# Moving four small loads to another engine's queue and reordering the first expert's loads in a LoRA mixture-of-experts kernel

## The chip, the cores and the metric

The kernel runs on one core of one Trainium2 chip. A core has TensorE (PE, with its weight loads as PEld), VectorE (DVE), ScalarE (ACT), GpSimd (POOL) and SyncE (SP); loads and stores are issued on the queues of SP, ACT and POOL and carried out by 16 DMA engines. The metric is the device time of one execution in microseconds (us); lower is better.

## The reference

The input is eight sequences of 256 rows of 256 numbers. Each goes through a gated retention layer against a context, and then through a mixture of eight experts, of which each row takes two:

```python
x = x + tanh(g_xattn) * xattn(layernorm(x), ctx, ctx, Wq, Wk, Wv)   # q, k rotated; (q k^T * decay) v
xf = layernorm(x)
gates = top2_normalised(softmax(xf @ Wg.T))                          # 8 experts, 2 per row
h1 = xf W1 + (xf A1) B1 + b1                                         # per expert, LoRA rank 16
h3 = xf W3 + (xf A3) B3 + b3
y_e = g W2 + (g A2) B2 + b2,   g = silu(h1) * h3
x = x + tanh(g_ffn) * sum_e gates_e * y_e
```

W1 and W3 are 512 x 256 per expert, W2 is 256 x 512, and the biases are drawn at random, so they count.

## The kernel before, in words

The kernel has two phases. In the **batch phase**, eight batch steps (`step(s, ...)` on each engine) compute the retention layer, one sequence per step. Beside it each step prepares the weights of one expert: the product of the LoRA factors is folded into the expert's weights. In the **tile phase**, 39 tiles of 128 gathered rows go through the experts (L617 to L644 on TensorE).

A step on TensorE (L519 to L571) has this order: keys of sequence s from its context `cx` (L529); from step 1 on the scores of s-1 (L493) and the first pair of fold products `units(0, 1)` (L471); the attention product (L514 to L516), which needs the masked scores `ret` that VectorE makes (L1213, L1214); transposes of the normalised rows `xn` (L482); fold products `units(2, 3)`; queries (L557); values (L566); fold products `units(4, 5)` (L475). Every engine runs its instructions in the order written, and so do the queues.

*The fold.* Each expert's weights come in six units of 128 x 512 (256 KB each), two per kind; the kinds 0, 1 and 2 are W1, W3 and W2. A unit lands in a `stage` buffer (L395), TensorE multiplies the LoRA rows `LS` (L471 or L475), VectorE adds the product to the stage (L1121), ScalarE rounds the sum into `WH` (L739), and GpSimd writes the rest into `WL` (L980). `LS[kind]` holds 48 LoRA rows (L387: 144 KB out of `WH`, where the split factors lie early on) and, for kinds 0 and 1, four rows that stand for the last weight row and the bias (L379) and, once, two unit rows (L372). A normalised row sums to zero, so the last weight row can be taken off all others, and a 1 in the last place carries the bias.

*The factors.* `lraw` is loaded kind by kind (`load_raw`, L413). VectorE subtracts the last column (L1169), ScalarE rounds into three parts (`round_factors`, L733 and L735), and rests are formed on VectorE (L1184, L1188) and GpSimd (L1006).

*The rows of last weights and biases.* Four loads of 16 KB (L420, L421: eight rows of 2 KB each) bring them into `last_raw`, 32 rows of 512. VectorE splits them into a rounded part and a rest, `last_rows` (`rows_of_last`, L1173 to L1178), at the end of its part of step 0.

*SyncE's queue* (L403 to L445) issues in this order: x and context of sequence 0, the projections and tables, `load_raw(0)`, a table, `load_raw(1)`, the four loads of last rows and biases, `load_raw(2)`, the mask, the gate weights, x and context of sequence 1, constants; then all six weight units of expert 0 (L429, L430); then, for each expert and kind, `load_factors` and (from expert 1 on) `load_weights`. `load_factors` makes the queue wait: for expert 0 on `s_last_rows` (L370), the unit rows, and the rounding and rests of this kind (L384 to L386); for later experts until TensorE is through with the LS buffer (L363). `load_weights` waits until GpSimd has freed the stage (L393).

*ScalarE* begins with the load of the two gate inputs (L709) and their tanh (L711), then the deviation of sequence 0 (L794, a square root), the normalised rows (L744), their transposes (L803). [...] It also loads x and context from sequence 2 on (L762, L763).

*GpSimd* clears the LS buffers and makes the unit rows (L990 to L1000), then takes its first step: key rotation (L985, L986), a factor rest, query rotation, another factor rest.

Of the kernel before, what the change touches and what calls it, by code (L numbers as in the profile page):

```python
# [25 lines left out]
F32 = mybir.dt.float32  # L26
# [52 lines left out]
def flamingo(nc, x, ctxT, wqkv, tables, mask, gates_in, w_all, lora, biases, wgT, ident_in, consts, out):  # L79
# [10 lines left out]
    with whole:  # L90
# [262 lines left out]
        def _(sp):  # L353
# [35 lines left out]
            def load_weights(s, u, kind):  # L389

                for m in (2 * kind, 2 * kind + 1):
                    n = s * UNITS + m
                    pos_wait(sp, s_wl, stage_last(n) + 1)  # L393
                    b = stage_of(n)
                    sp.dma_start(stage[b][:, :], w_all[s, m]).then_inc(s_stage[b], 16)  # L395

            def load_units(s, u, kind):

                load_factors(s, u, kind)
                if s > 0:  # L400
                    load_weights(s, u, kind)

            load_x(0)  # L403
            sp.dma_start(cx[0][:], ctxT[0]).then_inc(s_ctx[0], 16)
# [10 lines left out]
            load_raw(0)  # L415
            sp.dma_start(tab_q[:], tables[:, 0:2]).then_inc(s_qtab, 16)
            load_raw(1)
            for kind in range(2):
                rows = slice(2 * kind * E, 2 * (kind + 1) * E)
                sp.dma_start(last_raw[rows][0::2], w_all[:, 2 * kind + 1, P - 1, :]).then_inc(s_last_in, 16)  # L420
                sp.dma_start(last_raw[rows][1::2], biases[:, kind * HID:(kind + 1) * HID]).then_inc(s_last_in, 16)  # L421
            load_raw(2)
            sp.dma_start(msk, mask).then_inc(s_msk, 16)
            sp.dma_start(wg[:], wgT).then_inc(s_msk, 16)
# [3 lines left out]
            sp.dma_start(cst[:], consts).then_inc(s_cst, 16)  # L428
            for kind in range(KINDS):  # L429
                load_weights(0, 0, kind)  # L430
            for s in range(E - 1):
                for kind in range(KINDS):
                    load_units(s, s % 2, kind)

# [272 lines left out]
        @block.scalar  # L707
        def _(act):
            act.dma_start(gin[:], gates_in).then_inc(s_gin, 16)  # L709
            act.wait_ge(s_gin, 16)  # L710
            nc.scalar.activation(tg[:], gin[:], ACT.Tanh).then_inc(s_tg, 1)  # L711
            act.wait_ge(s_eps, 1)
# [264 lines left out]
        def _(pool):  # L977
# [20 lines left out]
            pool.wait_ge(s_unit_row, 2)  # L998
            nc.gpsimd.tensor_copy(unit_rows, unit_raw).then_inc(s_unit_row, 1)
            pool.wait_ge(s_unit_row, 3)  # L1000

            def factor_rest(kind):

# [111 lines left out]
        def _(dve):  # L1115
# [54 lines left out]
                dve.wait_ge(s_lsub, kind + 1)  # L1170
                nc.vector.memset(lraw[:, b - 1:b], 0.0).then_inc(s_ldiff, 1)

            def rows_of_last():  # L1173

                dve.wait_ge(s_last_in, 4 * 16)
                nc.vector.tensor_copy(last_rows[:, 0], last_raw).then_inc(s_last_hi, 1)
                dve.wait_ge(s_last_hi, 1)
                nc.vector.tensor_tensor(last_rows[:, 1], last_raw, last_rows[:, 0].bitcast(F32), ALU.subtract).then_inc(s_last_rows, 1)  # L1178

            def factor_rests(kind):  # L1180

                dve.wait_ge(s_lhi, kind + 1)
# [53 lines left out]
            def step(s, u, two, three):  # L1236
                b = s - 2
                weight = lambda m: add(s - 1, 1 - u, m)

                dve.wait_ge(s_kproj, s + 1)  # L1240
                pos_wait(dve, s_qT, 2 * s)
                rotate(pK, 2, 0)
                if s > 0:
                    variance(st1, mv1, s_mv1, early_sums[0])
                rotate(pK, 2, 1, s_krot)
                if s == 0:
                    lifted_factors(0)
                    lifted_factors(1)
                    factor_rests(0)
                else:  # L1250
                    dve.wait_ge(s_sd1, s + 1)
                    dve.wait_ge(s_xn, s)
                    shift(mv1, rs1, nm1, s_nm1, scale(sd1, rs1))
                if s == 1:
                    factor_rests(2)
                    dve.wait_ge(s_msk, 2 * 16)
                if two:
                    masked(s)
                    weight(0)
                    weight(1)  # L1260
                if three:
                    row_maxima(b, pL)
                    sorted_eight(b)
                    indices(b)
                if two:
                    if s == 1:
                        dve.wait_ge(s_tg, 1)
                    residual(s, xs[(s - 1) % XRING])
                    dve.wait_ge(s_x2, s)
                    n = sums(x2, st2)  # L1270
                    weight(2)
                    variance(st2, mv2, s_mv2, n)
                    weight(3)
                    if s == B - 1:
                        early_counts()
                    dve.wait_ge(s_sd2, s)
                    pos_wait(dve, s_xn2, s - 1)
                    shift(mv2, rs2, nm2, s_nm2, scale(sd2, rs2))
                if s == 0:
                    dve.wait_ge(s_qtab, 16)  # L1280
                dve.wait_ge(s_qproj, s + 1)
                dve.wait_ge(s_kT, 2 * (s + 1))
                rotate(pQ, 0, 0)
                rotate(pQ, 0, 1, s_qrot)
                if s == 0:
                    factor_rests(1)
                    rows_of_last()
                if s + 1 < B:
                    r = (s + 1) % XRING
                    dve.wait_ge(s_xload[r], 16 * ((s + 1) // XRING + 1))  # L1290
                    early_sums[0] = sums(xs[r], st1)
                    if two:
                        weight(4)
                        weight(5)
# [340 lines left out]
```

## Time and profile before

| | us |
|---|---|
| median of 3 runs | 327.74 (327.45 to 331.18) |
| the profiled execution | 328.52 |
| its span, first to last instruction | 326.7 |
| around the span | 1.8 |
| TensorE busy in the span | 297.4 (91%) |
| VectorE, ScalarE, GpSimd busy | 198.9, 203.5, 207.5 |
| mean granted TensorE clock | 0.968 of full |

Times in the rows are us from the start of the span. A busy TensorE is not TensorE at its peak, since matmuls are pipelined. The granted clock is 1.00 at 2.4 GHz and 0.50 at 1.2 GHz. "Idle before" is an engine's idle time ahead of an instruction, with what ended it; a q behind an engine's name (SPq, ACTq) means its sequencer, which issues loads.

### The profile page before, as it was taken

Reading aid. Unit: us, or ns where it says so; the run is one execution under the profiler, and the core shown is the slowest. Engines: PE = TensorE matmul, PEld = TensorE weight load, DVE = VectorE, ACT = ScalarE, POOL = GpSimd, SP = SyncE. Lnnn points to the kernel's source line nnn. Section 1 sums busy time; section 2 is a strip of 40 time slices with the busy share of each in tenths; the row PEclk is TensorE's granted clock in tenths of the full one; section 3 lists DMA queues with packets and bytes.
Section 4 is the critical chain, followed back from the end, with each engine's and each line's share of the span. In section 5 each row is a group of like instructions: output and inputs, shape, how many; then the busy total and the mean of one; then the engine's idle time right before and its main releaser. Section 6 shows DMA issues by size and latency. Waiting matters only on the chain.

```text
span 326.7 us, 7141 instructions
## 1 busy us (share of the span) xinstructions
PE 297.4 (91%) x1735; PEld 231.2 (71%) x1755; DVE 198.9 (61%) x533; ACT 203.5 (62%) x488; POOL 207.5 (64%) x253
## 2 busy tenths in 40 slices
PE   8659999999998698999999999999999999999960
PEld 3548778787887655876777777777777777777750
DVE  2957878789899985565666744444544534534430
ACT  5734656657779648768756656755755665665640
POOL 4637877878986069876576655755665665665241
PEclk9988997999999879999999999999999999999995
DMA  7987998998973247234243333322323223333100
GB/s 261 327 222 214 299 225 274 301 273 277 282 233 115 67 125 249 57 58 66 35 66 63 46 56 62 54 46 52 49 52 60 44 43 63 52 52 55 18 0 0
DMA packets 28073, 39.98 MB, mean 122 GB/s; under 512 B 6512, under 2 KB 16116, under 8 KB 27892
## 3 DMA queue, kind: packets, MB, share of 16 engines
q1 hardware_dynamic: 12244, 21.62, 22.5%
q0 software_dynamic: 7488, 9.36, 17.6%
q10 hardware_dynamic: 8304, 8.56, 8.4%
q8 instruction: 17, 0.28, 0.4%
q14 instruction: 20, 0.16, 0.2%
HBM read 27.35 MB, written 10.78 MB: 117 GB/s over the span
## 4 chain that ended last, share of the span: by engine, by line
PE 49%; DMA 2%; issue 1%; ACT 1%; POOLq 1%; ACTq 0%; DVE 0%; POOL 0%
PE bank L624 28%; PE bank L641 15%; PE bank L632 4%; PE bank L614 2%; DMA out<-ys,cols 2%; POOLq L90 1%; ACT L953 0%; ACT h L933 0%; ACT gh L875 0%; DVE ys L1544 0%; ACTq L907 0%; ACT ys L916 0%; POOLq L1037 0%; ACT gsel L893 0%; PE bank L693 0%
## 5 line engine op out<-in xcount | busy, mean ns | idle before, releaser
L1086 POOL DMA_INDIRECT out<-ys,cols x39 | 62.4, 1600 | 61.2 <-DVE ys L1544 45.9
L1533 DVE TENSOR_TENSOR gl<-bank,gh 128x512 fp32r<-128x512 f32 x39 | 27.0, 691 | 62.9 <-ACT gh L875 62.9
L875 ACT ACTIVATE gh<-bank 128x512 fp32r<-128x512 f32 x39 | 23.3, 597 | 65.3 <-PE bank L632 65.3
L624 PE MATMUL bank<-WH,xh 128*128 x156 | 55.5, 437 | 0.0
L980 POOL TENSOR_TENSOR WL<-stage,WH 128x512 bf16<-128x512 f32 x38 | 47.8, 1275 | 11.7 <-ACT WH L739 11.5
L1063 POOL DMA_INDIRECT xg<-xn_rows,colg x39 | 39.3, 1008 | 20.4 <-POOL colg L1041 10.3
L624 PE MATMUL bank<-WH,xl 128*128 x156 | 48.9, 395 | 0.0
L624 PE MATMUL bank<-WL,xb 128*128 x137 | 43.0, 384 | 1.3
L1538 DVE TENSOR_TENSOR g<-bank,h 128x512 f32<-128x512 f32 x39 | 26.9, 691 | 27.2 <-ACT h L933 27.2
L739 ACT ACTIVATE WH<-stage 128x512 fp32r<-128x512 f32 x38 | 23.0, 629 | 20.5 <-DVE stage L1121 13.4
L624 PEld LDWEIGHTS bank<-WH,xl 128*128 128x128 f32 x156 | 29.3, 188 | 6.5 <-DVE xl L1529 0.4
L641 PE MATMUL bank<-WH,gh 128*128 x156 | 32.0, 327 | 1.4 <-ACT gh L875 1.4
L641 PEld LDWEIGHTS bank<-WH,gh 128*128 128x128 f32 x156 | 23.9, 189 | 7.4 <-issue 2.1
L1121 DVE TENSOR_TENSOR stage<-bank,stage 128x512 f32<-128x512 f32 x38 | 24.5, 676 | 2.1 <-PE bank L471 2.1
L624 PEld LDWEIGHTS bank<-WH,xh 128*128 128x128 f32 x156 | 24.0, 190 | 1.8 <-issue 0.6
L879 ACT ACTIVATE gb<-gh 128x512 bf16<-128x512 f32 x39 | 24.9, 638 | 0.0
L641 PE MATMUL bank<-WH,gl 128*128 x156 | 24.8, 282 | 0.0
L632 PEld LDWEIGHTS bank<-ident,g 128*128 128x128 f32 x156 | 19.4, 141 | 7.5 <-DVE g L1538 0.2
L624 PEld LDWEIGHTS bank<-WL,xb 128*128 128x128 bf16 x156 | 9.0, 98 | 21.3 <-issue 21.3
L641 PE MATMUL bank<-WL,gb 128*128 x156 | 23.9, 276 | 0.0
L933 ACT ACTIVATE h<-bank 128x512 f32<-128x512 f32 x39 | 23.6, 606 | 0.0
L632 PE MATMUL bank<-ident,g 128*128 128x128 f32 x156 | 23.5, 273 | 0.0
(233 smaller groups left out, 646.9 us busy)
## 6 DMA issues: line engine op xcount, KB each, us to landing
stage<-w_all_in SPq DMA_DIRECT2D x38, 256.0 KB, 4.9
WL<-w_all_in SPq DMA_DIRECT2D x10, 256.0 KB, 3.6
LS<-WH SPq DMA_DIRECT2D x15, 144.0 KB, 3.9
xn_rows<-xn ACTq DMA_DIRECT2D x8, 255.0 KB, 3.7
out<-x ACTq DMA_DIRECT2D x7, 256.0 KB, 2.9
cx<-ctxT_in ACTq DMA_DIRECT2D x6, 256.0 KB, 6.6
lora_parts<-WH ACTq DMA_DIRECT2D x3, 432.0 KB, 6.8
LS<-lora_parts SPq DMA_DIRECT2D x9, 144.0 KB, 3.0
```

The source lines that it names most:

```text
L624: last = nc.tensor.matmul(dst[:, :], lhs[p][:, c * P:(c + 1) * P], W[:, bass.ds(e * (UNITS * UC) + (2 * kind + c) * UC, HID)], start=(part ...
L632: last = nc.tensor.transpose(pG[:, c * P:(c + 1) * P], g[:, c * P:(c + 1) * P], ident[:])
L641: last = nc.tensor.matmul(pY[:, 0:D], lhs[:, c * P:(c + 1) * P], W[:, bass.ds(e * (UNITS * UC) + 4 * UC + c * D, D)], start=(part == 0 and ...
L875: nc.scalar.activation(gh[:], pG[:, :], ACT.Copy).then_inc(s_gh, 1)
L879: nc.scalar.activation(gb[:], gh[:].bitcast(F32), ACT.Copy).then_inc(s_gb, 1)
L933: nc.scalar.activation(h1[:], pH1[:, :], ACT.Silu).then_inc(s_silu, 1)
L980: nc.gpsimd.tensor_tensor(w_dst(WL, s, m), stage[stage_of(s * UNITS + m)][:, :], w_dst(WH, s, m).bitcast(F32), ALU.subtract).then_inc(s_wl, 1)
L1063: nc.gpsimd.indirect_dma_start(out=xg[q][:], out_offset=None, in_=xn2_d[0:JA * P, :] if i < NA else xn2_d, in_offset=bass.IndirectOffsetOn ...
L1086: nc.gpsimd.indirect_dma_start(out=out_rows, out_offset=bass.IndirectOffsetOnAxis(ap=cols[:, i:i + 1], axis=0), in_=ys[p][:], in_offset=No ...
L1121: nc.vector.tensor_tensor(stage[b][:, :], pW[m % 2][:, :], stage[b][:, :], ALU.add).then_inc(s_add, 1)
L1533: nc.vector.tensor_tensor(gl[:], pG[:, :], gh[:].bitcast(F32), ALU.subtract).then_inc(s_gl, 1)
L1538: nc.vector.tensor_tensor(g[:], pH3[:, :], h1[:], ALU.mult).then_inc(s_g, 1)
```

## The change

SyncE no longer issues the four loads of last rows and biases; ScalarE's queue does, behind the gate load and ahead of the tanh. GpSimd splits the rows, with the same two operations as VectorE before, right behind the unit rows and ahead of its first key rotation; it waits for the four loads there. And SyncE issues the first expert's copies kind by kind: two weight units, then the LoRA rows of that kind, where before all six weight units came ahead of all LoRA rows.

```diff
             def load_units(s, u, kind):
                 load_factors(s, u, kind)
-                if s > 0:
-                    load_weights(s, u, kind)
+                load_weights(s, u, kind)
...
             load_raw(1)
-            for kind in range(2):
-                rows = slice(2 * kind * E, 2 * (kind + 1) * E)
-                sp.dma_start(last_raw[rows][0::2], w_all[:, 2 * kind + 1, P - 1, :]).then_inc(s_last_in, 16)
-                sp.dma_start(last_raw[rows][1::2], biases[:, kind * HID:(kind + 1) * HID]).then_inc(s_last_in, 16)
             load_raw(2)
...
             for kind in range(KINDS):
                 load_weights(0, 0, kind)
-            for s in range(E - 1):
+                load_factors(0, 0, kind)
+            for s in range(1, E - 1):
                 for kind in range(KINDS):
                     load_units(s, s % 2, kind)
...
             act.dma_start(gin[:], gates_in).then_inc(s_gin, 16)
+            for kind in range(2):
+                rows = slice(2 * kind * E, 2 * (kind + 1) * E)
+                act.dma_start(last_raw[rows][0::2], w_all[:, 2 * kind + 1, P - 1, :]).then_inc(s_last_in, 16)
+                act.dma_start(last_raw[rows][1::2], biases[:, kind * HID:(kind + 1) * HID]).then_inc(s_last_in, 16)
             act.wait_ge(s_gin, 16)
             nc.scalar.activation(tg[:], gin[:], ACT.Tanh).then_inc(s_tg, 1)
...
             pool.wait_ge(s_unit_row, 3)
+            pool.wait_ge(s_last_in, 4 * 16)
+            nc.gpsimd.tensor_copy(last_rows[:, 0], last_raw).then_inc(s_last_hi, 1)
+            pool.wait_ge(s_last_hi, 1)
+            nc.gpsimd.tensor_tensor(last_rows[:, 1], last_raw, last_rows[:, 0].bitcast(F32), ALU.subtract).then_inc(s_last_rows, 1)
+            pool.wait_ge(s_last_rows, 1)
...
-            def rows_of_last():
-
-                dve.wait_ge(s_last_in, 4 * 16)
-                nc.vector.tensor_copy(last_rows[:, 0], last_raw).then_inc(s_last_hi, 1)
-                dve.wait_ge(s_last_hi, 1)
-                nc.vector.tensor_tensor(last_rows[:, 1], last_raw, last_rows[:, 0].bitcast(F32), ALU.subtract).then_inc(s_last_rows, 1)
...
                 if s == 0:
                     factor_rests(1)
-                    rows_of_last()
```

## Rows read from the trace of the kernel before

**Rows 1.** Busy time by stretch: engines, PEclk (granted clock), DMA share, GB/s

```profile
16.00:28.00 12.00, 8.23 (x33) 6.54 (x32) 7.65 (x21) 3.65 (x7) 4.81 (x5) 0.86 0.81 218
66.00:78.00 12.00, 11.27 (x62) 9.41 (x62) 10.25 (x34) 7.97 (x17) 9.67 (x11) 1.00 0.97 289
160.00:200.00 40.00, 39.73 (x260) 30.77 (x263) 24.01 (x63) 24.75 (x66) 25.56 (x33) 1.00 0.34 55
```

**Rows 2.** Waits of TensorE, 0 to 120 us: total us, times, longest

```profile
PE bank L471 <- DMA LS<-WH: 3.6, 1, 3.6
```

**Rows 3.** Timeline of TensorE, steps 1 and 2: start us, us, instruction, idle before

```profile
15.16 1.99 PE L529 MATMUL bank<-cx,wq 128*128 128x256 f32 x8 [1.73 <-DMA cx<-ctxT_in]
...
22.06 0.73 PE L471 MATMUL bank<-LS 128*128 128x512 f32 x2 [3.59 <-DMA LS<-WH]
22.63 0.96 PE L514 MATMUL bank<-v,ret 128*128 128x256 f32 x2
...
26.83 1.99 PE L557 MATMUL bank<-xnT,wq 128*128 128x256 f32 x8 [0.18 <-ACT xnT L803]
...
36.27 0.70 PE L514 MATMUL bank<-v,ret 128*128 128x256 f32 x2 [0.16 <-DVE ret L1214]
...
39.04 2.00 PE L557 MATMUL bank<-xnT,wq 128*128 128x256 f32 x8 [0.31 <-ACT xnT L803]
```

**Rows 4.** Busy time by stretch, where the granted clock was 0.50

```profile
22.73:26.14 3.41, 3.41 (x12) 2.77 (x11) 1.89 (x3) 1.23 (x2) 2.11 (x2) 0.50 0.64 79
50.03:53.45 3.42, 3.42 (x12) 2.39 (x11) 3.03 (x13) 1.82 (x5) 3.18 (x4) 0.50 1.02 353
```

**Rows 5.** Timeline of SyncE's queue: when each load was issued

```profile
5.45 0.84 SPq L420 DMA_DIRECT2D WH<-w_all_in  x1
...
8.36 0.45 SPq L413 DMA_DIRECT2D WH<-lora_in  x1
...
10.27 0.43 SPq L358 DMA_DIRECT2D cx<-ctxT_in  x1
...
17.48 0.63 SPq L387 DMA_DIRECT2D LS<-WH  x1
```

**Rows 6.** Timeline of VectorE, 13 to 21 us

```profile
13.79 0.94 DVE L1176 CAST WH<-WH 32x512 fp32r<-32x512 f32 x1
14.77 1.10 DVE L1178 TENSOR_TENSOR WH<-WH 32x512 fp32r<-32x512 f32 x1
...
20.22 0.27 DVE L1214 TENSOR_TENSOR ret<-bank,WH 128x128 f32<-128x128 f32 x1
```

**Rows 7.** Busy time by stretch, with DMA share and GB/s, early step 0

```profile
7.00:10.00 3.00, 1.90 (x10) 1.27 (x9) 1.67 (x5) 1.85 (x4) 0.43 (x1) 1.00 1.01 374
10.00:13.00 3.00, 3.00 (x15) 2.64 (x15) 2.73 (x6) 3.00 (x6) 1.66 (x3) 1.00 0.85 265
```

**Rows 8.** Timeline of ScalarE, 1 to 12 us

```profile
1.19 1.28 ACT L711 ACT_TABLE_LOAD   x1 [1.19 <-PEq L1629]
...
4.91 1.28 ACT L794 ACT_TABLE_LOAD   x1 [0.75 <-DVE mv L1144]
...
10.59 0.92 ACT L735 ACTIVATE WH<-WH 128x512 fp32r<-128x512 f32 x2
```

**Rows 9.** Timeline of GpSimd, 3 to 16 us

```profile
3.95 0.28 POOL L999 CAST WH<-WH 2x128 fp32r<-2x128 f32 x1
9.57 0.72 POOL L985 TENSOR_TENSOR kT<-tA,tB 128x256 f32<-128x256 f32 x1 [5.35 <-DVE tB L1126]
...
12.32 1.27 POOL L1006 TENSOR_TENSOR WH<-WH 128x512 fp32r<-128x512 f32 x1 [1.34 <-ACT WH L733]
...
14.42 0.90 POOL L986 TENSOR_TENSOR qT<-tA,tB 128x256 f32<-128x256 f32 x1
```

**Rows 10.** Loads issued in 0 to 16 us on ScalarE's queue: KB, us to landing

```profile
cx<-ctxT_in ACTq DMA_DIRECT2D x1, 256.0 KB, 7.2
...
gin<-gates_in_in ACTq DMA_DIRECT2D x1, 1.0 KB, 3.2
```

## The prediction

> **What bounds the kernel now.** I read by stages first: the page's chain of waits reaches back only to the tile phase, so the table of stretches comes first. From 160 to 200 us TensorE is busy 39.73 of 40 us: the 39 tiles run at TensorE's pace, and they start when the batch steps before them have ended. A stretch of later batch steps, 66 to 78 us, is full too (11.27 of 12). The stretch from 16 to 28 us stands out: TensorE busy for only 8.23 of 12 us, with a granted clock of 0.86 [rows 1]. The reader should look for TensorE's waits there. In the first 120 us only two of them are for loads: 3.6 us for the LoRA rows LS [rows 2], and 1.7 us for the second context batch, cx (in brackets in rows 3). Where does their lateness come from?
>
> TensorE's order of time [rows 3] gives the frame. The key projection of step 1 starts at 15.16 after 1.73 us of waiting, so step 0 was through at 13.43; the LoRA products come at 22.06 after 3.59 us of waiting, so the scores were through at 18.47; the attention product starts at 22.63, the query projection at 26.83. Behind the long wait the clock is at its lower level: granted 0.50 (1.2 GHz) from 22.73 to 26.14 us [rows 4], behind the wait in which TensorE did nothing.
>
> SyncE's queue says why the data is late [rows 5]. It issues in order. The four small loads of last rows and biases hold it from 5.45 until the next load goes out at 8.36, 2.91 us; cx for step 1 is issued at 10.27 and the LoRA rows of the first expert's first kind at 17.48, since they stand behind all six weight loads and behind the rows that VectorE splits from 13.79 to 15.87 [rows 6].
>
> **The change, part by part.** All sums are on the profiled execution (328.52 us, of it 326.7 span; that is 0.78 us above the median of 327.74).
>
> *Four loads leave SyncE's queue.* All loads behind them are issued 2.91 us earlier: cx at 7.36 instead of 10.27. If its way took as long as before (15.16 - 10.27 = 4.89 us) it would be there at 12.25. But the DMA engines were moving 374 GB/s from 7 to 10 us at a busy share of 1.01, and 265 GB/s at 0.85 from 10 to 13 [rows 7]. The bytes ahead of cx are the same after the change; what an earlier issue can fill is the shortfall, 3 us x (374 - 265) = 327 KB, or 0.87 us at 374 GB/s. So cx lands between 12.25 (issue alone) and 15.16 (nothing gained), and I take 15.16 - 0.87 = 14.3. The Trainium skill, DMA: Bandwidth & Descriptors, section "Issuing engines are not separate DMA queues", speaks against the hope for more: it says that another issuing engine saves only the sequencer's time, as all share the same 16 DMA engines. Rows 7 agree in that the engines were full until 10 us; by the rule taken strictly the gain ends where the DMA engines have no idle time left, and the sum would be the 14.3 used here, not 12.25.
>
> *They join ScalarE's queue.* There they stand behind the gate load and ahead of the tanh, whose table load began at 1.19 and ended at 2.47 under cover of a wait [rows 8]. Costed as on SyncE, 2.91 us, they hold ScalarE from 1.19 to 4.10; then table load 1.28 to 5.38, tanh 0.2, and the second table load begins near 5.6, not 4.91. So the deviation, the normalised rows, the transposes, the query and the value projection of step 0 come 0.7 us later, and step 0 is through at 14.13 us. Bounds: nothing, if the issues cost ScalarE no time; 1.2 us, if each takes as long as the dearest of the four (4 x 0.84 [rows 5], 0.45 more than 2.91). The 0.7 is covered while cx lands no earlier than 14.13, so it costs nothing in my sum; without that cover it would be the whole 0.7. Together: the key projection of step 1 starts at 14.3, **0.86 us earlier**.
>
> *GpSimd splits the rows in place of VectorE.* On VectorE this was 0.94 + 1.10 us, done at 15.87; VectorE's next keys end on TensorE only at 15.16 + 1.99 = 17.15, so for VectorE itself this gives nothing. On GpSimd a copy of 512 columns lies between its cast of 128 columns (0.28) and the subtraction of 512 columns (1.27) [rows 9]; I take 0.9 from VectorE's own copy, and 1.27 for the subtraction: 2.2 us. GpSimd was idle for 5.35 us ahead of the key rotation at 9.57, so 2.2 us are hidden if the four loads have landed by 7.4. Issued by 4.10, with the 3.2 us that the gate load took on the same queue [rows 10], they land at 7.3. Later than that, up to 1.34 us is still hidden by GpSimd's idle time ahead of 12.32 [rows 9]. Behind this wait stand the key rotation, two factor rests and the query rotation, on which the scores of step 1 wait. With ScalarE 0.7 late the query rotation ends at 15.32 + 0.7 = 16.0, before the scores at 14.3 + 1.99 [rows 3].
>
> *Kind by kind.* The first expert's LoRA rows of kind 0 now stand behind two weight loads, not six, and behind rows that are ready at about 9.5. What remains is their rounding on ScalarE (ended at 11.51 [rows 8], now about 12.2): issued at about 12.3, not 17.48, 5.2 us earlier. Landing took 22.06 - 17.48 = 4.6 us before, hence 16.9. Behind this waiting issue on SyncE stand the weight loads of kinds 1 and 2, which now go out from about 12.9 on instead of 12.17; they are first added after the attention product, some 7 us later, which covers them.
>
> *What is late next.* TensorE ends its scores at 14.3 + 3.3 = 17.6 and finds LS there, or nearly. Next it needs the masked scores from VectorE. That chain (rotation of the keys, shift, a factor rest, mask) ended at 20.49, 5.33 us after the key projection began [rows 3, 6], and is unchanged: 14.3 + 5.4 = 19.7 for the attention product, against 22.63. So from the key projection to the attention product 5.4 instead of 7.47: **2.07 us**; of the wait of 3.6 us 1.5 remain under another name.
>
> *The clock.* From the attention product to the query projection took 26.83 - 22.63 = 4.20 us at the lower level. The same stretch of step 2, at full clock, took 39.04 - 36.27 = 2.77 [rows 3]. With TensorE idle for some 1.5 us in place of 3.6 I expect the full clock: **1.43 us**. Bounds: 0, if the lower level comes anyway, and 1.43.
>
> Sum: 0.86 + 2.07 + 1.43 = 4.36, say **4.4 us**. All later steps hang on TensorE's order and on queues that wait for it, so the shift should reach the end: 328.52 - 4.4 = 324.1 for the profiled execution, 327.74 - 4.4 = **323.3 us** on the median.
>
> **Rivals.**
> - *The earlier issue brings nothing* (the change doesn't do what it says there): cx lands at 15.16 as before, because the rings are full. For it: the share of 1.01 until 10 us. Against: the 0.85 behind it. Then only 2.07 + 1.43 = 3.5 remain: 324.2.
> - *A new slow-clock stretch* in place of the old one: TensorE idles 0.7 us longer in step 0 and still 1.5 us in step 1. For it: the lower level came behind an idle time before. Against: the wait of 1.7 us at 15.16 was not followed by one. Gain 4.4 - 1.4 = 3.0: 324.7.
> - *More than the first step:* the lower level from 50.03 to 53.45 us [rows 4] came at a time when the steps around it ran alike; shifted, it may stay away. It covers half as much work in 3.42 us, so up to 1.7 us: gain 6.1, 321.6; with term 1 at its upper bound also over 6.55.
> - *The DMA engines take it back:* their share is 0.97 from 66 to 78 us [rows 1]. If weights or stores come late once steps run 4.4 us ahead, half may go: 325.5. Against: after 22.06 us TensorE waits for no load until 120 us, only for engines; one such wait stands at 39.04 [rows 3].
> - *Slower:* GpSimd's wait. If the four loads are served only behind SyncE's backlog, they land with the first weights, about 16 us (the second key projection's data took until 15.16). The split (2.2), the key rotation (1.4), a factor rest (1.27) and the query rotation (1.8; GpSimd's two halves of a rotation take 0.72 or 0.90 each [rows 9]) then end 6.7 us later, at 22.7; VectorE's rotation of the next keys, planned for 16.3, waits for that: 6.4 us lost against 4.4 won, 329.7. It decides from a landing at about 14 us on. Against it: on ScalarE's queue 256 KB took 7.2 us beside the busiest stretch of weight loads [rows 10], so four of 16 KB, issued by 4.1, should be there by 11.3 at the worst, which costs 1.7. By the Trainium skill, the same page, section "Queues, rings and completion order", each DMA engine takes turns between the issuing engines' queues; by that rule the landing is early and this rival is off. Rows 10 agree as far as they go.
>
> **How the numbers follow.** Forecast 0.42, with its own range 322.3 to 324.6; the earlier issue worth nothing 0.17; a new slow-clock stretch 0.12; more than the first step 0.17; DMA takes it back 0.08; slower 0.04. The range from 320.3 to 326.6 leaves out the slower case, the worst of the DMA case and the best of the larger gain. Two per cent is 6.55 us, about what a measurement of this kernel can tell from no change: faster by more than that means below 321.2, half of the larger-gain case and a little of the forecast's tail, 0.16; slower by more than that takes two mishaps at once, 0.02; the rest, 0.82, lies within.
>
> **What would show it.** Key projection of step 1 at 14.0 to 14.6 us; the wait of 3.6 us for LS gone and in its place about 1.5 us for the mask (VectorE, ret); query projection of step 1 near 22.4; granted clock 1.00 through 16 to 28 us; the second table load on ScalarE near 5.6; GpSimd's key rotation still near 9.6. The forecast is wrong if TensorE still waits for LS, or if the key rotation starts after 11 us, or if step 2 begins 4 us earlier and the first tile doesn't.

## The result and the profile after

The changed kernel took 326.15 us (median of 12 runs), the kernel before 329.27 (12 runs): a ratio of 0.9865, with a 95% interval of 0.982 to 0.9911. A second measurement gave 326.0 (10 runs) against 329.93 (31 runs), ratio 0.9946 (0.9905 to 0.9987). All ratios and intervals of this document compare only runs within 1.5% of the fastest of their kernel, so they are not the quotients of the medians, which are of all runs (here 0.9905 and 0.9881). So the changed kernel is faster, by about half a per cent to one and a half. The profiled execution took 322.22 us (span 320.4, mean clock 0.979), 6.30 less than the one of before (328.52; 326.7; 0.968). Single executions of one kernel differ by several us (after: 322.22 to 330.66, and the profiled one is the shortest), so this pair of traces shows where time goes better than how much.

TensorE's timeline after the change, steps 0 to 2 (start, duration, instruction, idle time before it with what ended it):

```profile
9.43 0.63 PE L478 MATMUL bank<-ident,xn 128*128 128x128 f32 x4 [1.10 <-ACT xn L744]
...
12.64 1.89 PE L562 MATMUL bank<-wq,cx 128*128 128x256 f32 x8
14.36 1.89 PE L525 MATMUL bank<-cx,wq 128*128 128x256 f32 x8
...
17.53 0.71 PE L467 MATMUL bank<-LS 128*128 128x512 f32 x2
19.79 0.70 PE L510 MATMUL bank<-v,ret 128*128 128x256 f32 x2 [1.54 <-DVE ret L1212]
...
22.47 1.99 PE L553 MATMUL bank<-xnT,wq 128*128 128x256 f32 x8 [0.22 <-ACT xnT L803]
...
26.50 1.89 PE L525 MATMUL bank<-cx,wq 128*128 128x256 f32 x8
```

Against [rows 3]: the wait for cx and that of 3.59 us for LS are gone; what is left is 1.54 us for VectorE's masked scores. Key projection of step 1 at 14.36, not 15.16; attention product at 19.79, not 22.63; query projection at 22.47, not 26.83. Step 2 begins at 26.50, not 30.86.

Busy time by stretch (TensorE, its weight loads, VectorE, ScalarE, GpSimd, then granted clock, DMA share, GB/s) after the change:

```profile
4.00:7.00 3.00, 3.00 (x10) 1.53 (x9) 0.39 (x3) 2.49 (x3) 0.23 (x1) 1.00 0.94 281
7.00:10.00 3.00, 1.90 (x11) 1.24 (x9) 1.84 (x6) 1.67 (x4) 1.40 (x2) 1.00 1.00 352
10.00:13.00 3.00, 2.22 (x11) 1.96 (x11) 2.06 (x6) 2.83 (x5) 1.86 (x3) 1.00 1.05 396
16.00:28.00 12.00, 10.24 (x51) 8.28 (x50) 10.92 (x28) 6.98 (x14) 8.13 (x10) 1.00 1.02 280
```

From 16 to 28 us TensorE is busy 10.24 us where it was 8.23, and its clock is 1.00, not 0.86 [rows 1]. The clock over the whole span, in 40 slices (the page):

```profile
PEclk9999999999999599999999999999999999999995
```

The lower level shows only in the slice around 108 us and at the end; the stretch at 50 us [rows 4] is gone too, and with it step 3 is 1.80 us shorter (14.05 to 12.25; 0.73 of this is a wait of the kernel before that comes up again below). 4.36 from step 1 and 1.80 from there make up most of the 6.30.

ScalarE and its queue after the change:

```profile
1.19 1.28 ACTq L708 DMA_DIRECT2D WH<-w_all_in  x1
2.49 0.64 ACTq L709 DMA_DIRECT2D WH<-biases_in  x1
...
4.49 1.28 ACT L711 ACT_TABLE_LOAD   x1 [4.49 <-issue]
5.78 0.20 ACT L711 ACTIVATE tg<-gin 128x2 f32<-128x2 f32 x1
6.00 1.28 ACT L794 ACT_TABLE_LOAD   x1
7.30 0.30 ACT L794 ACTIVATE sd<-mv,eps_t 128x2 f32<-128x2 f32 x1
```

The table loads stand ahead of the tanh (L711) and of the square root (L794). The four issues hold ScalarE from 1.19 to 4.49, 3.30 us, and the second table load starts at 6.00 instead of 4.91 [rows 8]. TensorE pays for it at 9.43: 1.10 us of waiting for the normalised rows.

SyncE's queue after the change:

```profile
3.22 0.72 SPq L407 DMA_DIRECT2D wq<-wqkv_in  x1
...
8.64 0.43 SPq L358 DMA_DIRECT2D cx<-ctxT_in  x1
...
13.26 0.63 SPq L387 DMA_DIRECT2D LS<-WH  x1
```

cx goes out at 8.64 (before: 10.27) and the first LoRA rows at 13.26 (17.48) [rows 5].

GpSimd after the change:

```profile
8.51 0.60 POOL L1002 CAST WH<-WH 32x512 fp32r<-32x512 f32 x1 [4.29 <-DMA WH<-biases_in]
9.20 1.26 POOL L1004 TENSOR_TENSOR WH<-WH 32x512 fp32r<-32x512 f32 x1
10.54 0.72 POOL L985 TENSOR_TENSOR kT<-tA,tB 128x256 f32<-128x256 f32 x1
...
13.25 1.28 POOL L1011 TENSOR_TENSOR WH<-WH 128x512 fp32r<-128x512 f32 x1 [1.30 <-ACT WH L733]
```

The split costs 1.86 us and ends behind the time at which the key rotation ran before (9.57 [rows 9]); the rotation starts 0.97 us later, and GpSimd then still idles 1.30 us for ScalarE: nobody waited.

VectorE, the bound in step 1 after the change:

```profile
12.48 0.68 DVE L1186 TENSOR_TENSOR WH<-WH 128x512 fp32r<-128x512 f32 x1
...
18.07 1.12 DVE L1182 TENSOR_TENSOR WH<-WH 128x512 fp32r<-128x512 f32 x1
...
19.45 0.28 DVE L1212 TENSOR_TENSOR ret<-bank,WH 128x128 f32<-128x128 f32 x1
```

The masked scores end 5.4 us behind the start of the key projection, as before [rows 6]; a factor rest of 1.12 us stands just ahead of them. The rest in the first line ends at 13.16, and SyncE's queue waits for it before it issues the LoRA rows at 13.26.

### The profile page after: what moved, and what is told of

Read it like the earlier page. It is cut to its first block, busy times and chain, and to the rows that moved or that the text cites. A ratio compares the mean times of both kernels' runs of the same rounds, so it can differ in the third digit from the quotient of the medians.

```text
span 320.4 us, 7142 instructions
## 1 busy us (share of the span) xinstructions
PE 294.3 (92%) x1735; PEld 228.9 (71%) x1755; DVE 196.3 (61%) x531; ACT 203.4 (63%) x488; POOL 208.4 (65%) x255
## 4 chain that ended last, share of the span: by engine, by line
PE 68%; DVE 9%; ACT 6%; issue 6%; ACTq 5%; DMA 3%; POOLq 1%; POOL 0%; DVEq 0%
PE bank L620 32%; PE bank L637 16%; PE bank L628 5%; PE bank L553 4%; PE bank L562 4%; PE bank L610 3%; DMA xg<-xn_rows,colg 2%; ACTq L763 2%; DVE stage L1126 1%; ACT xnT L803 1%; PE bank L525 1%; ACT WH L739 1%; DMA out<-ys,cols 1%; DVE WL L1126 1%; ACTq L762 1%
```

## The experiments

**Which part carries the gain?** Four kernels, each with one part alone or one part taken back.

*The order alone.* The kernel before, with only the last edit:

```diff
...
             for kind in range(KINDS):
                 load_weights(0, 0, kind)
-            for s in range(E - 1):
+                load_factors(0, 0, kind)
+            for s in range(1, E - 1):
...
```

> The kernel before, with the first expert's copies issued kind by kind and nothing else. My theory (a chain: the LoRA rows go out only when the split rows are there): VectorE still ends the split at 15.9 us, so the LoRA rows of kind 0 are still issued near 17.5; only the four weight loads ahead of them are gone, so they land up to 0.7 us sooner. Attention product of step 1 at 22.0 to 22.6, time 0 to 0.7 us below the kernel before. Rival (the order of issue alone carries the gain): attention product near 20, 3 us or more below.

Measured: 330.21 us, ratio 1.0041 (0.9984 to 1.0099): no gain. The rows that the queue waits for come from VectorE as late as before, so the queue stops there. SyncE's queue in this run:

```profile
18.19 0.63 SPq L387 DMA_DIRECT2D LS<-WH  x1
```

*All but the order.* The changed kernel with all six weight loads ahead of the LoRA rows again:

```diff
             for kind in range(KINDS):
                 load_weights(0, 0, kind)
-                load_factors(0, 0, kind)
+            for kind in range(KINDS):
+                load_factors(0, 0, kind)
```

> The changed kernel with all six weight loads of expert 0 ahead of its LoRA rows, as before. Theory: the LoRA rows are issued at about 14.3 us but stand behind 1.5 MB of weights in the same rings and land at 20 to 21.5; TensorE waits some 3 us for them, the slow clock follows, and the query projection of step 1 comes at 24.5 to 26; time 0.5 to 2 us below the kernel before. Rival (the split and its place carry the gain, the order is an ornament): query projection at 22.5, 4.4 us below.

Measured: 328.48 us, ratio 1.0004 (0.9952 to 1.0056). The part of the gain that was expected isn't there. TensorE in this run:

```profile
21.83 1.22 PE L468 MATMUL bank<-LS 128*128 128x512 f32 x2 [3.83 <-DMA LS<-WH]
```

The LoRA rows were issued at 14.95, 2.5 us earlier than in the kernel before, and landed only at 21.83, 6.9 us later, behind 1.5 MB of weights. The clock was at its lower level from 21.11 to 27.94, and the query projection came at 27.16.

*The loads on SyncE's queue again,* with the split on GpSimd and the order kept:

```diff
             load_raw(1)
+            for kind in range(2):
+                rows = slice(2 * kind * E, 2 * (kind + 1) * E)
+                sp.dma_start(last_raw[rows][0::2], ...)
+                sp.dma_start(last_raw[rows][1::2], ...)
...
```

> The changed kernel with the four small loads back on SyncE's queue; GpSimd still splits, copies kind by kind. Theory: context of step 1 at 15.2 as before, rows landed at 11.0, so GpSimd's key rotation starts near 13 and its query rotation ends near 17.4, which sets VectorE's rotation; attention product near 20.8, query projection near 23.6: 3.2 us below the kernel before, 1.2 us above the changed one. Rival (the slower case of the prediction: GpSimd's wait eats the gain): query projection at 26 or later, no gain.

Measured: 327.89 us, ratio 1.0002 (0.9964 to 1.004). GpSimd and TensorE in this run:

```profile
12.58 0.91 POOL L1002 CAST WH<-WH 32x512 fp32r<-32x512 f32 x1 [8.35 <-DMA WH<-biases_in]
```

```profile
15.21 3.28 PE L529 MATMUL bank<-cx,wq 128*128 128x256 f32 x8 [2.14 <-DMA cx<-ctxT_in]
19.47 1.55 PE L493 MATMUL bank<-qT,kT 128*128 128x256 f32 x8 [0.98 <-POOL qT L986]
```

Here the rival "GpSimd's wait" of the prediction can be seen small: the rows landed at 12.58, the key rotation moved to 14.91, and the scores waited 0.98 us for GpSimd. The wait of 2.14 us for cx was followed by the lower clock, so that the key projection took 3.28 us instead of 1.99; a wait of 2.66 us for cx in the run with the shorter fill, below, was not. The attention product came at 23.03, no earlier than before, and the query projection at 25.71, 1.1 us earlier. So the other two edits without the move of the loads brought nothing that the total shows.

*The split on VectorE again,* with the loads on ScalarE and the order kept:

```diff
                 if s == 0:
                     factor_rests(1)
+                    rows_of_last()
...
-            pool.wait_ge(s_last_in, 4 * 16)
-            nc.gpsimd.tensor_copy(last_rows[:, 0], last_raw).then_inc(s_last_hi, 1)
...
```

> The changed kernel with the split back on VectorE at the end of its step 0; loads on ScalarE's queue, copies kind by kind. Theory: the split ends near 16.9 us, the LoRA rows of kind 0 are issued near 18.4 and land near 22.5, VectorE's key rotation starts near 17.6; attention product near 23, query projection 26 to 27: 0 to 1 us below the kernel before. Rival (VectorE had room, the split's engine does not matter): query projection near 23, 4 us below.

Measured: 331.04 us (4 runs), ratio 1.0123 (0.9964 to 1.0281). SyncE's queue stops for VectorE's rows:

```profile
17.42 0.74 SPq L372 DMA_DIRECT2D LS<-WH  x1
```

TensorE waited 4.05 us for LS. So the three edits are links of one chain, not three gains: early landing, an engine with nothing else to do, and a queue in which the rows aren't behind 1.5 MB. Each one taken out costs the whole gain, as far as the total can show it (the lower ends of the three intervals are 0.9952 to 0.9964). The loads alone and the split alone were not run.

**The clock.** The kernel before, with TensorE kept at work in its wait for LS by products whose result nobody reads:

```diff
                 if two:
                     scores(s)
+                if s == 1:
+                    keep_clock(7, wq[:, 1].rearrange("p c d -> p (c d)"))
                 units(0, 1)
```

> The kernel before, with seven matmuls of no use (128x512, f32, on the key weights) in TensorE's wait for the LoRA rows of step 1; nothing else moves. It measures the clock term alone. Theory: attention product at 22.6 to 22.9 us as before, granted clock 1.00 from 22.7 to 26.1, query projection at 25.4 (1.4 earlier), time 1.4 us below the kernel before. Rival (another engine sets that stretch, the slow clock is only seen beside it): query projection at 26.8, no gain.

Measured: 330.30 us, ratio 1.0068 (1.0019 to 1.0118). The fill (14 products in the trace) took 6.17 us, more than the wait of 3.59, and held up the LoRA products by itself: the attention product came at 24.78. But from there to the query projection it took 2.58 us, not 4.20. A shorter fill (8 products):

```diff
-                    keep_clock(7, wq[:, 1].rearrange("p c d -> p (c d)"))
+                    keep_clock(4, wq[:, 1].rearrange("p c d -> p (c d)"))
```

> The kernel before, with TensorE kept at work in its wait for LS by 16 idle-purpose products fewer than the longer fill had (four groups in place of seven; the longer fill took 6.17 us, so this one about 3.5), and nothing else. Theory (the lower clock after the wait is worth about 1.4 us by itself): the fill runs from 18.4 to about 21.9, the LoRA products still start near 22.1 (LS is as late as before), the attention product near 22.7, the query projection 2.6 to 2.8 us behind it (before: 4.20), so near 25.4, and the steps behind it come 1.4 us earlier; total about 1.4 us below the kernel before if no other slow stretch changes. Rival (the lower clock comes whatever TensorE does there, or it costs nothing because ScalarE is the bound): the query projection again 4 us behind the attention product, no gain.

Measured: 329.27 us, ratio 0.9967 (0.9914 to 1.0019). TensorE in this run:

```profile
18.84 3.60 PE L453 MATMUL bank<-wq 128*128 128x512 f32 x8
23.31 0.73 PE L471 MATMUL bank<-LS 128*128 128x512 f32 x2 [0.87 <-DMA LS<-WH]
23.88 0.60 PE L514 MATMUL bank<-v,ret 128*128 128x256 f32 x2
...
26.47 1.99 PE L559 MATMUL bank<-xnT,wq 128*128 128x256 f32 x8 [0.22 <-ACT xnT L805]
```

With work in place of most of the idling the stretch takes 2.59 us instead of 4.20: 1.6 us are the clock's. In the total it can't be told from nothing: cx came 0.55 us later in this execution and LS 1.25, and a lower-clock stretch stood at 38.28 to 41.70 instead of 50.

**What bounds the first step after the change?** The changed kernel once more:

> The changed kernel once more, for a second profile. Theory: query projection of step 1 near 22.5 us and granted clock 1.00 from 16 to 28 us again, since these follow from the order of work; a stretch of slow clock in a later batch step may come or not, and the span moves by up to 1.8 us with it. Rival (the whole 6.3 us between the two profiled spans belongs to the change): a span of 320 to 321 again.

Measured: 326.0 us, as said above; the trace is of its shortest execution, 324.43. TensorE in this run:

```profile
15.11 1.99 PE L525 MATMUL bank<-cx,wq 128*128 128x256 f32 x8 [0.58 <-DMA cx<-ctxT_in]
...
32.38 1.03 PE L501 MATMUL bank<-wg,xn2T 128*128 128x8 f32 x8 [0.99 <-ACT xn2T L756]
```

This time cx was late by 0.58 us (issued at 8.94, landed 6.1 later), and step 2 took 13.07 us, with a wait of 0.99 for ScalarE's transposed rows. The query projection of step 1 came at 23.27, not near 22.5. The clock was 1.00 through all batch steps again.

*One load in place of four:* the 32 rows laid together by the host, one load of 64 KB at the same place on ScalarE's queue.

```diff
-            for kind in range(2):
-                rows = slice(2 * kind * E, 2 * (kind + 1) * E)
-                act.dma_start(last_raw[rows][0::2], ...)
-                act.dma_start(last_raw[rows][1::2], ...)
+            act.dma_start(last_raw, last).then_inc(s_last_in, 16)
...
```

> The changed kernel with the 32 rows laid out as one array, so one load of 64 KB on ScalarE's queue in place of four. ScalarE gets its time back: second table load at 4.9 us, step 0 through at 13.2. Theory (the context of step 1 is bound by the bytes ahead of it): it lands near 14, the key projection of step 1 starts at 13.9 to 14.2, query projection 22.0 to 22.4, 0.1 to 0.4 us below the changed kernel. Rival (ScalarE's delay was the bound): key projection at 13.2 to 13.4, 1 us below the changed kernel.

Measured: 325.71 us, ratio 0.9943 (0.988 to 1.0005): in the total no different from the changed kernel (326.0 on the same chip). Step 1 went against my theory. TensorE, and the stretch 4 to 13 us, in this run:

```profile
13.00 2.00 PE L525 MATMUL bank<-cx,wq 128*128 128x256 f32 x8
...
18.53 0.70 PE L510 MATMUL bank<-v,ret 128*128 128x256 f32 x2 [1.54 <-DVE ret L1209]
...
42.84 1.03 PE L501 MATMUL bank<-wg,xn2T 128*128 128x8 f32 x8 [0.88 <-issue]
...
56.42 1.03 PE L501 MATMUL bank<-wg,xn2T 128*128 128x8 f32 x8 [1.44 <-issue]
```

```profile
4.00:7.00 3.00, 3.00 (x13) 1.90 (x12) 0.93 (x6) 1.84 (x3) 2.08 (x3) 1.00 1.03 368
7.00:10.00 3.00, 1.95 (x11) 1.29 (x10) 1.61 (x4) 1.90 (x4) 0.75 (x2) 1.00 1.01 398
10.00:13.00 3.00, 3.00 (x15) 2.36 (x14) 2.62 (x7) 2.75 (x6) 1.66 (x2) 1.00 1.06 395
```

And the stretch 4 to 7 us in the kernel before:

```profile
4.00:7.00 3.00, 3.00 (x12) 1.66 (x11) 1.23 (x7) 1.74 (x3) 0.23 (x1) 1.00 1.06 380
```

cx was there by 13.00, since the key projection follows the values without a wait. From 4 to 7 us the DMA engines moved 368 GB/s, where the four loads of eight rows left them at 281 with a busy share of 0.94. The engines were busy, so it was hardly for want of issued loads: the four small loads slow the transfers beside them. In the kernel before, the shortfall stood at 10 to 13 us [rows 7]; over the whole of 4 to 13 us the engines moved 340 GB/s before, 343 in the changed kernel, and 387 here. How the small loads do this no run shows. But the first tile started at 116.54, 0.83 us *later* than in the changed kernel (0.54 earlier than in its second trace), though the query projection of step 1 was 1.26 earlier. Steps 3 and 4 took 13.01 and 13.58 us, with TensorE waiting ahead of the gate products (0.88, 1.44), its products of the transposed rows `xn2T` with the gate weights `wg`. ScalarE in step 4 of this run:

```profile
52.46 1.93 ACTq L760 DMA_DIRECT2D cx<-ctxT_in  x1
54.43 0.63 ACT L736 ACTIVATE WH<-stage 128x512 fp32r<-128x512 f32 x1 [3.23 <-issue]
...
55.72 0.60 ACT L753 ACTIVATE xn2T<-bank 128x512 f32<-128x512 f32 x1
```

ScalarE issues the next context, then rounds units 4 and 5, then copies the transposed rows that TensorE waits for. In these traces the length of a step goes with the time of that issue, in the kernel before too (its step 3 also holds the lower-clock stretch of [rows 4]):

| run, step | issue of cx, us | step, us |
|---|---|---|
| before, 2 to 4 | 1.04, 1.56, 1.01 | 12.21, 14.05, 12.41 |
| changed, 2 to 4 | 1.33, 1.09, 1.04 | 12.47, 12.25, 12.42 |
| changed again, 2 to 4 | 1.98, 1.08, 1.03 | 13.07, 12.23, 12.42 |
| one load, 2 to 4 | 1.53, 1.59, 1.93 | 12.63, 13.01, 13.58 |

So this wait is not new. The kernel before, from ScalarE's queue, from TensorE's timeline in step 3, and from TensorE's waits in 0 to 120 us (total us, times, longest):

```profile
44.56 1.56 ACTq L763 DMA_DIRECT2D cx<-ctxT_in  x1
...
47.91 1.03 PE L505 MATMUL bank<-wg,xn2T 128*128 128x8 f32 x8 [0.73 <-issue]
...
PE bank L505 <- issue: 3.2, 4, 2.0
```

The last line is the second largest of those waits, next to the one of [rows 2]; 2.0 of it fall ahead of the last gate products, behind step 7. The lower clock often follows this wait. Over all 14 traces of this document nine lower-clock stretches lie in steps 2 to 5, and each begins 0.8 to 2.4 us behind the start of gate products that had waited 0.73 to 1.42 us; four other waits, of 0.88 to 1.44 us, were followed by none. No run tests this by itself.

*The context first:* the changed kernel with x and cx of sequence 1 issued ahead of `load_raw(2)`, the mask and the gate weights.

```diff
             load_raw(1)
+            load_x(1)
+            load_ctx(1, 1)
             load_raw(2)
...
-            load_x(1)
-            load_ctx(1, 1)
```

> The changed kernel with x and context of step 1 issued ahead of the third factor load, the mask and the gate weights: 520 KB fewer ahead of the context. Theory: it lands near 12.7 us, but step 0 on TensorE is through only at 14.3 because of ScalarE's delay, so the key projection starts at 14.3 and the time is that of the changed kernel within 0.3 us: two bounds lay on one another. Rival (the load alone is the bound): key projection near 12.9, 1.4 us below the changed kernel.

Measured: 325.89 us, ratio 0.9916 (0.9873 to 0.996). The key projection started at 14.36 right behind the values, as expected from step 0; but the scores then waited 0.93 us for GpSimd's query rotation, and the query projection came at 23.42, later than in the changed kernel (the trace is of the longest of the ten executions, 329.35 us). cx was issued at 6.76, 1.9 us earlier, and took 7.2 us instead of 5.5: it landed at 13.96 against 14.1. So the bound by the load was hardly moved, and the two bounds were not told apart.

**Was the gain given back behind step 1?** The run with one load, and in ScalarE's part the copy of the transposed rows and the next deviation ahead of the roundings of units 4 and 5 and of the factor stores:

```diff
                 if three:
                     act.wait_ge(s_xn2Tp, s - 1)
                     copy_xn2T(pT)
...
+                if three:
+                    weight_hi(s - 2, u, 4)
+                    weight_hi(s - 2, u, 5)
+                    if s <= 4:
+                        store_factors(s - 2)
...
-                if two:
-                    if s < B - 1:
-                        hi(4, 5)
-                    if s <= 3:
-                        store_factors(s - 1)
```

(The store of the last rows moves with them.)

> The changed kernel with one load of 64 KB for the 32 rows (as in the run with one load) and, new, ScalarE's order in steps 2 to 7: the copy of the transposed rows (xn2T) and the deviation of the next step now come ahead of the two roundings of units 4 and 5 and of the factor stores; nothing is left out. In the run with one load step 1 was 1.4 us ahead of the changed kernel, and the first tile 0.8 us behind it; steps 3 and 4 took 13.0 and 13.6 us there, with TensorE waiting 0.88 and 1.44 us ahead of the gate products, where ScalarE's issue of the next context took 1.59 and 1.93 us (1.04 to 1.09 in the changed kernel). Theory (the gain was given back on ScalarE: its copy xn2T stands behind the issues and two roundings): the wait ahead of the gate products goes or falls below 0.3 in every step, steps 2 to 4 take 12.0 to 12.5 us each, the first tile starts at 113 to 114.5 us, total 2 to 3 us below the run with one load. Rival (the DMA engines are full and data would be late elsewhere): the wait moves to LS, cx or stage loads or to VectorE's masked scores, steps 3 and 4 still take 13 us or more, and the total does not change.

Measured: 321.43 us (320.48 to 323.23, 4 runs), ratio 0.9782 (0.9711 to 0.9853): faster than the kernel before, by 8.1 us between the medians, where the changed kernel gained 3.1 and 3.9 (the two were not run side by side). TensorE in this run:

```profile
15.47 1.55 PE L489 MATMUL bank<-qT,kT 128*128 128x256 f32 x8 [0.64 <-POOL qT L983]
...
41.28 0.95 PE L501 MATMUL bank<-wg,xn2T 128*128 128x8 f32 x8
...
53.05 0.95 PE L501 MATMUL bank<-wg,xn2T 128*128 128x8 f32 x8
```

No wait is left ahead of the gate products in these steps; steps 2 to 4 take 11.61, 11.77 and 11.44 us although the issue of cx still took 1.51, 1.34 and 0.47. The first tile starts at 113.50.

The same edit of ScalarE's order in the changed kernel itself, with its four loads:

```diff
                     copy_xn2T(pT)
...
+                if three:
+                    weight_hi(s - 2, u, 4)
+                    weight_hi(s - 2, u, 5)
...
```

> The changed kernel with its four loads as they are, and ScalarE's order in steps 2 to 7 as in the run with the roundings behind (xn2T and the next deviation ahead of the roundings of units 4 and 5 and of the factor stores). Theory (two separate limits: the loads set step 1, ScalarE's order sets the steps behind it): step 1 as in the changed kernel, key projection near 14.4 and query projection near 22.5; steps 2 to 4 take 11.5 to 12.2 us each as with one load, so the first tile 2.5 to 4 us earlier than in the changed kernel, 112 to 113.5, and the median 322 to 323.5, about one us above the run with one load. Rival (the gain of the run with the roundings behind came from the single load, the order only helps with it): steps 2 to 4 still take 12.3 us or more and the total is that of the changed kernel, 326.

Measured: 323.36 us (4 runs), ratio 0.9796 (0.9725 to 0.9867), 6.7 us below the median of the kernel before. Steps 2 to 4 took 12.00, 12.03 and 11.85 us, so the order works without the single load. Step 1 missed what was expected: a lower-clock stretch stood at 11.81 to 15.22 in this execution, and the key projection came at 16.05; the first tile at 116.32.

Last, in the run with the roundings behind, VectorE's rest of the third kind (L1182 above) moved behind the masking in step 1:

```diff
                 if s == 1:
-                    factor_rests(2)
                     dve.wait_ge(s_msk, 2 * 16)
                 if two:
                     masked(s)
                     weight(0)
                     weight(1)
+                if s == 1:
+                    factor_rests(2)
```

> The kernel of the run before this one (one load, xn2T ahead of the roundings), and VectorE's rest of the third kind (1.13 us) in step 1 moved behind the masking and the weights of the fold, nothing left out. Theory (in step 1 the masked scores are the bound, and the rest stands 1.13 us ahead of them on VectorE): the attention product of step 1 starts 4.4 to 4.6 us behind the key projection instead of 5.5, TensorE's wait for VectorE there falls from 1.54 to about 0.5, and step 2 starts about 1 us earlier; first tile 1 us earlier. Rival (another engine is right behind it, ScalarE's xnT or the third kind's LS): attention starts earlier, but the query projection or the fold of units 4 and 5 waits, and step 2 starts less than 0.4 us earlier.

Measured: 322.21 us (4 runs), ratio 0.9792 (0.9725 to 0.986), no different from the run without the move. The step itself went as planned:

```profile
18.58 0.70 PE L510 MATMUL bank<-v,ret 128*128 128x256 f32 x2 [0.39 <-DVE ret L1209]
...
42.62 1.03 PE L501 MATMUL bank<-wg,xn2T 128*128 128x8 f32 x8 [0.56 <-issue]
```

The attention product came 4.94 us behind the key projection (6.09 without the move). Step 1 took 11.74 us instead of 12.80, but it started 0.71 us later in this execution, so step 2 began only 0.35 us earlier; step 3 then took 13.09 us, and the first tile came at 114.98, 1.48 us later than without the move.

## Why the prediction was right, and where it was not

**The time.** The forecast was 323.3 us against 327.74, a ratio of 0.9865. That the first measurement gave this very ratio is luck: the second gave 0.9946, and the medians give 0.9905 and 0.9881. In us the medians of 326.15 and 326.0 lie within the range of 320.3 to 326.6 but above the forecast's own 322.3 to 324.6, in the main because the kernel before had medians of 329 to 330 in these runs.

**The three terms.** In the profiled pair each came out within 0.1 us: key projection 0.80 earlier (0.86 was said), key projection to attention product 5.43 us in place of 7.47, so 2.04 (2.07), attention to query projection 2.68 in place of 4.20, so 1.52 (1.43). The sum is 4.36, and step 2 begins 4.36 us earlier. The wait for the mask, 1.54 us, was named with its size (1.5). The sizes of the first pair of traces are not a law: in the second trace of the changed kernel the key projection came at 15.11, and the first term was nearly nothing, as the first rival has it. Over the traces the key projection began at 15.02 to 15.71 with the four loads on SyncE (five traces), and at 14.36 to 15.11 with them on ScalarE and the context in its old place (four; 16.05 in a fifth, with a lower-clock stretch in step 0).

**The clock term** was the least sure, and the runs show its size: with TensorE at work in most of that wait, the stretch took 2.58 and 2.59 us in place of 4.20. In both traces of the changed kernel the clock stayed at its upper level behind the 1.54 us.

**"What an earlier issue can fill is the shortfall"** gave the right size by luck. From 7 to 13 us the DMA engines did move 3 x (352 + 396 - 374 - 265) = 327 KB more, the amount counted; but from 4 to 7 us they moved 281 GB/s in place of 380, so that over 4 to 13 us both kernels moved nearly the same, 340 and 343 GB/s. The shortfall was not filled: the four small loads made it, and the change carried it to an earlier place. So what made cx land 0.9 us earlier is open. The rule weighed there (the Trainium skill, DMA: Bandwidth & Descriptors, "Issuing engines are not separate DMA queues") says that loads issued by any engine run on the same 16 DMA engines. This case agrees: on another engine's queue the four loads cost the transfers as much as before. But 14.3 us, where the gain was to end, was no bound: with one load cx was used at 13.00.

**"0.7 is covered while cx lands no earlier than 14.13".** ScalarE's delay was mis-sized: the four issues took 3.30 us, not 2.91, so the second table load began 1.09 us late, not 0.7 (it stays within the bound of 1.2). And the cover was used up: step 0 was through at about 14.3, cx landed at 14.1. The two bounds meet. The context issued first lifted neither (it landed at 13.96) and brought nothing; one load, which lifts both, brought 1.36 us on the key projection.

**The issue times** were taken as unchanged, 2.91 us earlier for all. Three of SyncE's six issues took 0.58 to 0.72 us while ScalarE issued its four, and later ones up to 0.91, in place of 0.43 to 0.45, so cx went out at 8.64, not 7.36. The LoRA rows went out at 13.26, not 12.3, because the sum ends with ScalarE's rounding and leaves out VectorE's rest behind it, which ended at 13.16. The slack in front of the LoRA products, which were there at 17.53 just in time, took it.

**GpSimd's wait** had its slack: the rows landed at 8.5, not 7.3, the key rotation came at 10.54, not 9.6, within the 1.34 us that [rows 9] left. The run with the loads on SyncE shows the rival's mechanism at a landing of 12.58: 0.98 us at the scores. The landing of 14 from which it would have decided never came.

**"The shift should reach the end"** held in the traces: step 2 began 4.36 and 3.56 us earlier than in the kernel before, and the first tile 5.88 and 4.51 (121.59 before, 115.71 and 117.08 after). The medians show less, 3.1 (329.27 to 326.15) and 3.9 us, but with executions up to 8 us apart it is not shown that this is below 4.4. Both traces are of the shortest execution of their series; where the longer ones lose their time no trace shows, except that they mostly have the lower mean clock (0.979 at 322.22 us, 0.966 at 330.66).

What the prediction overlooked is a second limit, which was there before the change. It followed only TensorE's waits for loads, and so passed over those ahead of the gate products, where ScalarE is late. Its issue of the next context takes 1.0 to 2.0 us there, and a step grows by up to 1.3 us. That this is the place is shown by the order of ScalarE's instructions alone: it takes steps 2 to 4 to 11.4 to 12.0 us, with the four loads as with one. (In the last run, with this order too, step 3 still took 13.09 us, behind issues of 1.33 and 0.78.) The change neither made this limit nor removed it: TensorE's waits ahead of the gate products in steps 2 to 5 come to 1.22 us in the kernel before, and 0.88 and 1.48 in the changed one. With one load they come to 3.03 and use up what step 1 gained. In the profiled pair the lower-clock stretch in step 3 stayed away besides, the third rival: 6.30 us, where it said 6.1. Why such stretches come in one execution and not in the next is open, and with it most of the spread of single executions.

**The parts.** The prediction priced the split and the order in one term and the loads in another. The runs say that none of the three edits has a price of its own: without any one of them the total is that of the kernel before, as far as the intervals tell.

## What to carry to other kernels

A late load usually has a chain behind it (where it is issued, what its queue waits for, what lies ahead of it on the way): follow it to the end before you price one link, and try the links together. Read the waits that are not for loads too, and read them again once a step has been made earlier: an engine that both issues loads and computes holds up its next result by the time of its issues, so what others wait for belongs ahead of what nobody waits for yet. And lay many short rows together before you move them: here that alone made step 1 1.4 us earlier, though not yet the total.

## What was unexpected of the hardware

- Four loads of eight rows of 2 KB each held the issuing engine for 1.28, 0.64, 0.63 and 0.63 us and took the transfers beside them down to 281 GB/s; one load of the same 64 KB was issued in 0.45 us, with 368 GB/s in the same stretch.
- An issue can be slower while another queue issues: three of SyncE's six took 0.58 to 0.72 us while ScalarE issued its four small loads, and none more than 0.44 in the same stretch with one load. The issue of one 256 KB context took ScalarE 0.44 to 2.00 us in these traces; what sets it was not tested.
- An earlier issue is a landing earlier by less: 10.27 + 4.8, 8.64 + 5.5, 6.76 + 7.2 us for the same load.
- Behind a table load of 1.28 us there was no further idle time: in the changed kernel the tanh began 0.01 us after it, the square root 0.02.
